# Second expert layer: from all experts for every token to blocks of chosen token-expert pairs

## The reference

```
logits = flat @ router_w.T ; probs = softmax(logits)
topk_probs, topk_idx = top_k(probs, 2) ; topk_probs /= sum(topk_probs) + 1e-9
gates[n, e] = topk_probs where e was chosen, else 0
h = silu(flat @ w1[e].T) * (flat @ w3[e].T)      # 8 experts, 128 -> 341
y = h @ w2[e].T                                  # 341 -> 128
out[n] = sum_e gates[n, e] * y[n, e]
```

## Time and profile before

| | us |
|---|---|
| median of 3 runs (lowest, highest) | 553.89 (552.29, 556.23) |
| span of the profiled execution | 552.8 |
| PE busy, of the span | 487.0 (88%) |
| DVE, ACT, POOL busy | 388.4, 268.6, 117.0 |
| DMA moved | 25.79 MB |
| mean granted TensorE clock | 0.948 |

### The profile page before, as it was taken

How to read it: one execution, slowest core, us unless ns; L and a number is a source line. 1 busy time by engine, 2 the same in 40 slices (tenths; PEclk the granted TensorE clock), 3 DMA queues, 4 the chain that set the end, 5 groups by cost and what they waited for, 6 DMA issues and landing times.

```text
span 552.8 us, 6153 instructions
## 1 busy us (share of the span) xinstructions
PE 487.0 (88%) x1884; PEld 300.3 (54%) x1884; DVE 388.4 (70%) x709; ACT 268.6 (49%) x443; POOL 117.0 (21%) x171
## 2 busy tenths in 40 slices
PE   5496789868799989999799999899898998998996
PEld 3332545435356744556344444335466886776896
DVE  1997989766576832257648959767877967778674
ACT  5988787678675521032431222202225556565553
POOL 4000000000010000000000000885203554546564
PEclk9689589989799999989999999979998999999999
DMA  8880000000000010000000000332031221312340
GB/s 285 264 245 6 0 0 0 1 1 0 2 0 1 2 51 1 0 2 1 0 0 1 3 26 1 101 88 63 4 93 53 72 67 58 96 60 48 65 91 15
DMA packets 23640, 25.79 MB, mean 47 GB/s; under 512 B 2565, under 2 KB 18960, under 8 KB 23604
## 3 DMA queue, kind: packets, MB, share of 16 engines
q1 hardware_dynamic: 23604, 25.36, 16.1%
HBM read 24.61 MB, written 0.74 MB: 46 GB/s over the span
## 4 chain that ended last, share of the span: by engine, by line
PE 55%; DVE 24%; ACT 10%; issue 8%; DMA 1%; SPq 0%; POOLq 0%; DVEq 0%; POOL 0%; ACTq 0%
PE bank L1292 10%; PE bank L943 7%; PE bank L944 6%; PE bank L945 6%; PE bank L1122 4%; PE bank L1240 3%; DVE pr_ring L1887 3%; PE bank L1083 2%; PE bank L1281 2%; DVE y_units L1433 2%; DVE y_units L1444 2%; PE bank L1209 2%; PE bank L972 2%; DVE hr_ring L1703 2%; PE bank L1210 2%
## 5 line engine op out<-in xcount | busy, mean ns | idle before, releaser
L1292 PE MATMUL bank<-pr_ring,hW 128*128 128x512 f32 (+3 forms) x198 | 95.0, 565 | 6.6 <-DVE pr_ring L1887 6.0
L1887 DVE SCALAR_TENSOR_TENSOR pr_ring<-adjT,regR,bank 128x512 f32<-128x512 f32 (+3 forms) x99 | 64.7, 680 | 30.6 <-PE bank L1281 28.9
L1900 DVE TENSOR_TENSOR adjT<-bank,adjT 128x512 f32<-128x512 f32 (+1 forms) x66 | 41.3, 626 | 29.1 <-ACT bank L892 28.8
L1292 PEld LDWEIGHTS bank<-pr_ring,hW 128*128 128x128 f32 (+1 forms) x198 | 35.0, 194 | 36.6 <-DVE pr_ring L1887 18.8
L943 PE MATMUL bank<-z3hi,w13hi 128*128 128x512 f32 (+4 forms) x132 | 50.8, 385 | 3.6 <-DVE adjT L1900 3.6
L892 ACT ACTIVATE bank<-bank 128x512 f32<-128x512 f32 (+1 forms) x66 | 35.0, 531 | 36.3 <-PE bank L945 36.1
L944 PE MATMUL bank<-z3lo,w13hi 128*128 128x512 f32 (+4 forms) x132 | 48.9, 371 | 0.0
L945 PE MATMUL bank<-z3hi,w13lo 128*128 128x512 f32 (+4 forms) x132 | 48.8, 370 | 0.0
L604 POOL TENSOR_TENSOR prr_ring<-adjT,adjTr 128x512 fp32r<-128x512 f32 (+4 forms) x34 | 36.5, 1073 | 56.4 <-ACT adjTr L881 51.6
L972 PE MATMUL bank<-y_units,msg 128*128 128x512 f32 (+3 forms) x66 | 34.5, 655 | 15.7 <-DVE y_units L1454 15.7
L1083 PE MATMUL bank<-hr_ring,W2s 128*128 128x512 f32 (+1 forms) x96 | 45.5, 561 | 0.0
(11 more groups left out here) (270 smaller groups left out, 1025.3 us busy)
## 6 DMA issues: line engine op xcount, KB each, us to landing
adjT<-rows SPq DMA_DIRECT2D x16, 256.0 KB, 3.5
stage<-in_w SPq DMA_DIRECT2D x8, 341.0 KB, 2.9
adjT<-in_adjT SPq DMA_DIRECT2D x1, 2560.0 KB
adjT<-in_adjT SPq DMA_DIRECT2D x1, 1650.0 KB
adjT<-in_adjT SPq DMA_DIRECT2D x3, 512.0 KB, 6.9
adjT<-rows SPq DMA_DIRECT2D x8, 165.0 KB, 4.2
adjT<-in_adjT SPq DMA_DIRECT2D x1, 1024.0 KB
W1f<-in_W SPq DMA_DIRECT2D x1, 1024.0 KB, 11.7
```

Of the source, the lines that this page charges most:

```text
L1292: nc.tensor.matmul(B_ACC[:, 0:w], hW[0:r, j, k * P:(k + 1) * P], ring[0:r, 0:w], start=(k == 0 and j == 0), stop=(k == K - 1 and j == T - ...
L1887: nc.vector.scalar_tensor_tensor(out=pr_ring[0:r, 4 + p % R_RING, 0:w], in0=adjT[0:r, j, cols(c)], scalar=g_col[0:r, j, k:k + 1], in1=B_F[ ...
L1900: nc.vector.tensor_tensor(halves(sg, w), halves(B_H1[h_bank(q)][0:r, 0:w], w), gate_buf(n)[0:r, :, :], ALU.mult).then_inc(s["s_gated"], 1)
```

## The change

The second expert layer computes only chosen pairs. Per group of tokens (group 0 is chunk 0, group 1 is chunks 1 and 2) each pair gets a row ("slot") in a DRAM table sorted by expert. PE counts the pairs ahead of each (`prefix`), DVE turns the counts into slots and, for each block of 128 rows, into the block's first row and the place of its expert's weights (`route_slots`). POOL scatters the normalised token rows into the table with indirect DMAs (`send`), two per tile of tokens. The number of blocks is fixed at what any routing may need: 15 for group 0, 21 for group 1, NB = 36. A block is loaded by SP at a row number read from SBUF, turned by PE, sent through w1, w3, silu, product, three transposes and w2 in full float32, and stored by SP to a second table. After the blocks of a group POOL gathers two result rows per token (`gather`), and DVE adds them with their gates to x in token-major form (`combine`). Before all that SP fills the four tables with zeros. The weights are loaded whole (`wall`, 4.4 MB) and not split. The last update of chunk 2, its layernorm and its routing stand before and among the first ten blocks.

```diff
+HP = -(-H1 // 3)
+HT = [(k * HP, min(HP, H1 - k * HP)) for k in range(3)]
+WALL = 2 * H1 + len(HT) * P
+GROUPS = [(0, 4), (4, T)]
+CAP = [b - a for a, b in GROUPS]
+BLOCKS = [(2 * (min(N, b * P) - a * P) + E * (P - 1)) // P for a, b in GROUPS]
+TABLE = [E * n + m for n, m in zip(CAP, SPARE)]
+XRING = 4
+YRING = 4
+HOLD = 4
+PRE_PE = [("gates", 1, 2), ("prefix", 1), ("mid", 1, 2)]
+PRE_DVE = [("ranks", 4), ("picks", 4), ("mid", 1, 2), ("slots", 4), ("blend", 1, 2), ("add", 1, 2)]
+PE1 = {0: [("xtok", 0)], 1: [("mean", 3, 2)], 2: [("var", 3, 2)], 3: [("xtok", 1)], 4: [("logits", 5)], 5: [("ztok", 2)], 8: [("prefix", 2)], 10: [("xtok", 2)]}
...
@@ sync (SP)
+            for g in range(2):
+                n = TABLE[g]
...
+                for table in (xg_d[g], yg_d[g]):
+                    sp.dma_start(table..., zeros[:, 0:n * P // k]...).then_inc(s["tables_in"], 16)
...
-            for e in range(E):
-                at(sp, "w13_lo", e - 1)
...
+            def block_load(b):
+                g, i = BLOCK[b]
+                if i == 0:
+                    sp.wait_ge(s["list_set"], g + 1)
+                    sp.wait_ge(s[f"sent{g}"], 32 * (GROUPS[g][1] - GROUPS[g][0]))
+                at(sp, "xt_ps", b - XRING + 1)
+                row = sp.value_load(row_no[0:1, b:b + 1], min_val=0, max_val=(TABLE[g] - 1) * P)
+                sp.dma_start(xblk[:, b % XRING, :], xg_d[g][bass.ds(row, P), :]).then_inc(s[f"xb_in{b % XRING}"], 16)
+
+            def block_store(b):
+                g = BLOCK[b][0]
+                sp.wait_ge(s["y_set"], b + 1)
+                row = sp.value_load(row_no[0:1, b:b + 1], min_val=0, max_val=(TABLE[g] - 1) * P)
+                sp.dma_start(yg_d[g][bass.ds(row, P), :], yblk[:, b % YRING, :]).then_inc(s[f"y_out{b % YRING}"], 16)
+
+            for b in range(NB):
+                block_load(b)
+                if b >= HOLD:
+                    block_store(b - HOLD)
...
@@ gpsimd (POOL)
+            pool.memset(zeros[:, :], 0.0).then_inc(s["zpad_set"], 1)
...
-            pool.wait_ge(s["r_set"], SPLIT_AFTER)
-            for e in range(E):
...
+            def send(c):
...
+                for t in tiles(c):
+                    for j in range(2):
+                        pool.indirect_dma_start(xg_d[g], bass.IndirectOffsetOnAxis(slot[0:r, t, j:j + 1], 0), ztok[0:r, t, :], None
+                                                ).then_inc(s[f"sent{g}"], 16)
+            def gather(g):
+                last = sum(BLOCKS[:g + 1])
+                for i in range(YRING):
+                    pool.wait_ge(s[f"y_out{i}"], 16 * len(range(i, last, YRING)))
+                for t in range(*GROUPS[g]):
+                    for j in range(2):
+                        pool.indirect_dma_start(picked_y[0:r, t, j, :], None, yg_d[g], bass.IndirectOffsetOnAxis(slot[0:r, t, j:j + 1], 0)
+                                                ).then_inc(s[f"got{g}"], 16)
...
@@ vector (DVE)
+            def combine(t):
...
+                    at(dve, f"got{g}", 32 * (GROUPS[g][1] - GROUPS[g][0]))
+                link(nc.vector.scalar_tensor_tensor(out=answer[0:r, t, :], in0=picked_y[0:r, t, 0, :], scalar=wab[0:r, t, 0:1],
+                                                    in1=x3tok[0:r, t, :], op0=ALU.mult, op1=ALU.add))
...
+                for task in PRE_DVE:
+                    gat_side(task)
+                for b in range(2):
+                    block_turned(b)
+                for b in range(NB):
+                    nc.vector.tensor_tensor(hbuf[:, b % 2, 0:H1], hbuf[:, b % 2, 0:H1], B_H3[b % 2][:, 0:H1], ALU.mult).then_inc(s["m_set"], 1)
+                    if b + 2 < NB:
+                        block_turned(b + 2)
+                    if b > 1:
+                        block_out(b - 2)
...
@@ tensor (PE)
+                for task in PRE_PE:
+                    gat_side(task)
+                pe.wait_ge(s["wall_in"], 80)
+                for b in range(2):
+                    block_turned(b)
+                for b in range(NB):
+                    bases[b] = pe.value_load(wall_at[0:1, b:b + 1], min_val=0, max_val=(E - 1) * WALL)
+                    up(b, bases[b])
+                    if b + 2 < NB:
+                        block_turned(b + 2)
+                    if b:
+                        hidden_turned(b - 1)
+                    if b > 1:
+                        down(b - 2, bases.pop(b - 2))
+                    for task in PE1.get(b, []):
+                        gat_side(task)
+                hidden_turned(NB - 1)
+                for b in (NB - 2, NB - 1):
+                    down(b, bases.pop(b))
```

More of the change, by code:

```diff
@@ L9 @@
 I32 = mybir.dt.int32
+U32 = mybir.dt.uint32
 ALU = mybir.AluOpType
@@ L23 @@
 H1 = 341
[L24 to L42, removed]
+HP = -(-H1 // 3)
+HT = [(k * HP, min(HP, H1 - k * HP)) for k in range(3)]
+WALL = 2 * H1 + len(HT) * P
+GROUPS = [(0, 4), (4, T)]
+GROUP_OF = [0, 1, 1]
+CAP = [b - a for a, b in GROUPS]
+BLOCKS = [(2 * (min(N, b * P) - a * P) + E * (P - 1)) // P for a, b in GROUPS]
+SPARE = [n - -(-2 * (min(N, b * P) - a * P) // P) for n, (a, b) in zip(BLOCKS, GROUPS)]
+TABLE = [E * n + m for n, m in zip(CAP, SPARE)]
+BLOCK = [(g, i) for g in range(2) for i in range(BLOCKS[g])]
+NB = len(BLOCK)
+XRING = 4
+YRING = 4
+HOLD = 4
 K = 3
@@ L154 @@
[L154 to L160, removed]
@@ L599, in _ @@
[L599 to L605 removed]
+            pool.memset(before[:, :], 1.0).then_inc(s["tables_const"], 1)
@@ L607, in build @@
+            pool.wait_ge(s["tables_in"], 64)
+            for c in range(C):
+                send(c)
+            for g in range(2):
+                gather(g)
         CONSTS = 2 + 2 + PARTS + 2
@@ new lines, in prefix @@
+            def prefix(c):
+                at(pe, "tables_const", 7)
+                at(pe, "picked", c + 1)
+                take_side("pos_read", c + 1)
+                own, first = list(tiles(c)), GROUPS[GROUP_OF[c]][0]
+                n = len(own)
+                for i, t in enumerate(own):
+                    r = rows(t)
+                    nc.tensor.matmul(B_SIDE[:, i * E:(i + 1) * E], before[0:r, :], mk[0:r, t, :], start=True, stop=(t == first))
+                    for q in range(first, t):
+                        nc.tensor.matmul(B_SIDE[:, i * E:(i + 1) * E], oneb[:, 0:1].to_broadcast([P, P]), mk[:, q, :], start=False, stop=(q == t - 1))
+                end = own[-1] + 1
+                for q in range(first, end):
+                    r = rows(q)
+                    mm = nc.tensor.matmul(B_SIDE[:, n * E:(n + 1) * E], oneb[0:r, 0:1].to_broadcast([r, P]), mk[0:r, q, :],
+                                          start=(q == first), stop=(q == end - 1))
+                mm.then_inc(s["pos_ps"], 1)
@@ new lines, in hidden_turned, with down @@
+            def hidden_turned(b):
+                at(pe, "m_set", b + 1)
+                at(pe, "ht_set", b)
+                for k in range(3):
+                    mm = nc.tensor.transpose(B_HT[0:HP, k * P:(k + 1) * P], hbuf[:, b % 2, k * HP:(k + 1) * HP], ident[:, :])
+                mm.then_inc(s["ht_ps"], 1)
+            def down(b, base):
+                at(pe, "ht_set", b + 1)
+                at(pe, "y_set", b)
+                for k, (_, r) in enumerate(HT):
+                    mm = nc.tensor.matmul(B_Y[:, 0:P], hturned[0:r, b % 2, k * P:(k + 1) * P],
+                                          walls[0:r, bass.ds(base + 2 * H1 + k * P, P)], start=(k == 0), stop=(k == 2))
+                mm.then_inc(s["y_ps"], 1)
@@ L2011, in _ @@
                         if c == 0:
-                            for task in [("ranks", C), ("weights", C), ("turn", C)]:
+                            for task in [("ranks", C), ("picks", C), ("slots", C), ("weights", C)]:
                                 gat_side(task)
```

495 lines of the change are left out of this document (245 added, 250 removed).

## The result

The changed kernel takes **671.75 us** (median of 4 runs, 668.83 to 673.03) against 553.83 for the kernel before on the same chip: ratio 1.212, 95% interval 1.207 to 1.217. Slower, as forecast; 664 was forecast, with a range of 618 to 692, which holds it. The profiled execution has a span of 670.4 us.

What follows compares the result with a forecast made beforehand. PE alone was taken to bound the old expert layer. Forecast: block 5 turned at 440, 30 times 6.05, drain 12, store 3.5, gathers 17.6, combination 4.8, output 3.2: span 662.6, plus 1.1, 664 us; range 618 to 692.

Steps and rivals of the forecast that it cites:

- The wait that takes over: Block loop: SP's store waits for an older result and holds up the next load; 6.05 us a block.
- PE busy under 60%: Block stretch: a sign that would show the forecast wait, with PE busy under 60% there.
- SP's 1.4 us: Block loop, SP: two register loads at 0.4, one issue 0.37, six short register instructions 0.2 together; sum 1.4 us.
- The load: Block loop: a 64 KB row block's DMA from issue to landing, taken as 2.3 us, ends 2.0 and 2.9.
- The clock: Block loop: PE's granted clock, full giving 5.5 us a block and half 6.6; the middle, 6.05, was taken.
- The rival "stays at half": Block loop: PE's clock stays at half, 6.9 us a block for 30 blocks, 692 us in all; chance 0.20.
- The period: Block loop: 6.05 us a block, 30 times, from the turn of block 5 to that of block 35.
- Ahead of the blocks: Attention loop's end to early blocks: first up-projection near 424 us, block 5 turned near 440.
- The drain: Loop's end: rest of iteration 33, two iterations without a load, last product and two down-projections; 12 us taken.
- The gathers: Tail: POOL gathers 14 times at 1.1 us each plus 2.2 to land, 17.6 us.
- Costed at nothing: Whole kernel: work expected to be covered: zero fill (13.4 MB), weights (4.4 MB), group 1's sends, group 0's gather and combination.
- The rival "PE sets the pace": Block loop: loads run ahead enough, 2.7 us a block gives 554 us, 3.3 gives 576; chance 0.10.

Runs made afterwards that it cites:

- The first two experiments: Changed kernel with each block's store issued six loads later instead of four (`HOLD = 6`), 574.4 us; then five loads later (`HOLD = 5`), 581.2 us.
- the experiment on the clock: Changed kernel plus eight spare bfloat16 matmuls, read by nobody, behind each up-projection from block 11 on: 654.3 us, ratio 1.180.
- the two runs with 28 blocks and `HOLD = 6`: 12 and 16 blocks instead of 15 and 21, stores six loads later: against the 574.4 us kernel, 560.4 us; against the 562.45 us one, 552.5 us.
- the first experiment: Changed kernel with each block's store issued six loads later instead of four (`HOLD = 6`): 574.4 us, ratio 1.036.

## Why the prediction held, and where its sizes were off

- **The wait that takes over** was named rightly: store before load in SP's queue, so that a result of one iteration gates a load that the next one needs. The first two experiments show it as the cause and not a companion: no byte and no matmul changed, and 97 us went. Of the signs that the prediction named, the waits for `xblk` and `y_set` and the period came as said; PE busy under 60% did not. It was busy for 59 to 71% of the windows above: its work per block had been priced at full clock, and at the lower one the same records last longer.
- **SP's 1.4 us** is the term that was mis-sized most. It was 1.99 us on average (0.80 + 1.19). The register load itself was overestimated (0.27 instead of 0.4), while the time around it wasn't in the sum at all. The six short register instructions, "taken as 0.2 together", had their price from no row of the trace, as the prediction says itself; a whole register-addressed DMA costs 0.7 to 0.8 us beyond one with a fixed address, twice per block.
- **The load** landed 1.8 us after its issue (1.88 to the next turn), not 2.3, and the copy took 0.29, not 0.34. Nothing is left for the 0.15 of handing over either.
- **The clock** was taken midway between full and half, 0.55 us of the 1.1 between the two ends. PE's part of the loop was 2.09 us on average, nearer to the 2.4 of half than to the 1.33 of full, and the experiment on the clock puts its share at 0.9. The rival "stays at half" was right for some stretches, not for the loop.
- **The period** came out well by luck: against the terms above, PE's 1.87 (the middle), 0.34, 1.4, 2.3 and 0.15, the measured ones differ by +0.22, -0.05, +0.59, -0.42 and -0.15. That is +0.19, 6.24 instead of 6.05. The forecast of the period was better than its parts.
- **Ahead of the blocks** 440 was forecast for the turn of block 5, 439.46 measured. That it fits to half a microsecond is luck: in two other traces with the same first blocks that turn stands at 434.57 and 441.16. **The drain** to the last copy took 10.4 us, 12 forecast. **Store and landing** 3.6, 3.5 forecast.
- **The gathers** cost 1.25 us each and 3.9 from the last one's start to the first combination, 20.5 in all; 17.6 forecast, from POOL rows of other instructions. **The combination** 4.7 as forecast, and the output 4.4 instead of 3.2.
- Added up against the forecast span of 662.6: -0.5 + 5.8 (30 periods) - 1.6 + 0.1 + 2.9 - 0.1 + 1.2 = +7.8, which is the 670.4 measured.
- **Costed at nothing:** the zero fill rightly (sent twice, no change). That group 1's sends would be the next wait, were the blocks three times as quick, is what the two runs with 28 blocks and `HOLD = 6` show, 10.9 and 10.8 us. Group 0's gathers "inside the loop" weren't quite free even under the wait for SP: two turns stand 7.50 and 7.11 us apart while they are issued, where the neighbours have 6.4, some 2 us in all. Where PE sets the pace they leave it idle for 5 us.
- **The rival "PE sets the pace"** had 2.7 us a block, with 0.4 for the register load; at 2.26 PE hides that load. With the order mended the kernel lands at 574, inside this rival's 554 to 576. The change would pay below 2.65 us a block only if little stood beside the blocks: from the first turn to the last (422.8 to 530.8) 108 us pass in the first experiment, of which 35 periods of 2.26 are 79. The other 29 are chunk 2's layernorm and route, the sends and the gathers, which the rival had as 4.

## What to carry to other kernels

A ring of buffers only buys distance if the queue that fills it isn't held by an instruction that waits for this round's result: write down for each queue, in order, what every instruction waits for, and count in iterations. When a loop waits on one such chain, price each hop including what surrounds it, and take the time from issue to issue, not from the listed instructions. And a wait that a profile names after an engine may be a disturbance from elsewhere: move the suspect (the combinations here), and if the wait stays in place, look at what runs at that moment on queues that nobody waits for.

## What the runs showed of the hardware

- A DMA whose address comes from a register on SP costs mostly 0.72 to 0.79 us more in the queue than one with a fixed address (0.75 and 1.12 us where the fixed ones have 0.03 and 0.37), although its three listed instructions last 0.44 us together.
- An indirect DMA of 128 rows of 512 bytes keeps POOL mostly 0.94 us (at most 1.02) and the next one follows 0.30 later, whether 8, 14 or 22 stand in a row; the two of the last tile, which has 74 rows, take 1.35 each.
- Eight such gathers left PE idle for 5 us in a loop that doesn't wait for them, sixteen for 14 us of 26.
- PE's full clock came back with spare work: 1.00 instead of 0.69 in the same window, and the kernel got shorter by 17.5 us. From the turn to the copy the same instructions take 1.36 us at full clock and 2.43 at half.
- A register load on PE between independent matmuls costs nothing that shows: 2.26 us a block, where the matmuls alone had been summed to 2.3 from the rows of the kernel before.
- The same instructions don't start at the same time in every trace: the first turn stands between 415.4 and 422.8 us in twelve traces with the same attention stage. A difference of a few us between two single traces says little.
